# Routed experts: from 24 tiles of 256 slots with stationary weights to 39 tiles of 128 slots with stationary rows

## The reference, cut to what matters

```
probs = softmax(x @ router_w.T);  topk_w, topk_idx = top_k(probs, 2)   # x: 2048 x 512, 8 experts
topk_w = topk_w / sum(topk_w);    combine[token, expert] = topk_w
for each expert:                  # gate_w, up_w: 512 x 352; down_w: 352 x 512
    out = silu(x @ gw) * (x @ uw) @ dw
    acc = acc + combine[:, expert] * out
shared = silu(x @ s_gate_w + s_gate_b) * (x @ s_up_w + s_up_b) @ s_down_w + s_down_b
return acc + shared
```

## Time and profile before

| | us |
|---|---|
| median of 3 runs (2123.87 to 2126.93) | 2124.59 |
| the profiled execution | 2125.85 |
| its span, first to last instruction | 2124.1 |
| TensorE busy in the span | 1867.7 |

### The profile page before, as it was taken

One profiled execution on the slowest core, in us unless ns is written; L12 is line 12 of the kernel. 1 busy time (PEld: TensorE's weight loads), 2 busy tenths in 40 slices (PEclk: granted clock), 3 DMA queues, 4 the chain that ended last, 5 costly groups with the idle time before them and its releaser, 6 DMA issues. The chain is left out here.

```text
span 2124.1 us, 30631 instructions
## 1 busy us (share of the span) xinstructions
PE 1867.7 (88%) x11050; PEld 1539.2 (72%) x11050; DVE 1301.2 (61%) x2410; ACT 919.1 (43%) x1755; POOL 667.4 (31%) x482
## 2 busy tenths in 40 slices
PE   4999996965999679999999999984895999998597
PEld 4999984752445368888888888873674888987475
DVE  5343424777787447677767767755533777776244
ACT  3333323764667445465455536533212555553211
POOL 2110102214556321222213212102363666653322
PEclk8999997987999879999999999997997999999798
DMA  5010103541011331222213212003005777773434
GB/s 198 21 39 20 37 32 140 188 169 60 11 41 41 119 130 51 70 90 80 70 59 112 70 50 95 6 1 107 21 1 172 232 229 236 240 225 122 120 107 129
DMA packets 131028, 209.03 MB, mean 98 GB/s; under 512 B 9990, under 2 KB 69670, under 8 KB 130790
## 3 DMA queue, kind: packets, MB, share of 16 engines
q1 hardware_dynamic: 119228, 170.89, 24.0%
q0 software_dynamic: 11696, 36.77, 6.0%
HBM read 169.84 MB, written 37.79 MB: 98 GB/s over the span
## 5 line engine op out<-in xcount | busy, mean ns | idle before, releaser
L1311 POOL TENSOR_TENSOR a_rq<-a_ssq,a_mhalf 128x4 f32<-128x4 f32 x64 | 65.1, 1017 | 413.6 <-DVE a_ssq L1433 413.6
L69 PE MATMUL bank<-a_xT_hi,a_wq_lo 128*128 128x512 f32 (+1 forms) x384 | 145.0, 378 | 21.7 <-PEq L47 18.1
L1394 ACT ACTIVATE a_pT_hi<-bank 128x512 fp32r<-128x512 f32 x128 | 69.6, 599 | 192.9 <-PE bank L1548 192.9
L2222 DVE TENSOR_TENSOR m_h_lo<-m_hf,m_h_hi 128x256 fp32r<-128x256 f32 (+1 forms) x72 | 122.6, 1703 | 36.6 <-ACT m_h_hi L2176 36.6
L70 PE MATMUL bank<-a_xT_lo,a_wq_hi 128*128 128x512 f32 (+1 forms) x384 | 139.4, 363 | 0.0
L71 PE MATMUL bank<-a_xT_hi,a_wq_hi 128*128 128x512 f32 (+1 forms) x384 | 139.4, 363 | 0.0
L1388 ACT ACTIVATE a_scores<-a_scores,a_nmax 128x256 f32<-128x256 f32 x256 | 127.1, 503 | 27.9 <-DVE a_nmax L1448 27.6
L69 PE MATMUL bank<-a_wo_hi,a_oT_lo 128*128 128x512 f32 x320 | 128.2, 401 | 2.7 <-DVE a_oT_lo L368 1.4
L71 PE MATMUL bank<-a_wo_hi,a_oT_hi 128*128 128x512 f32 x320 | 126.5, 395 | 0.0
L70 PE MATMUL bank<-a_wo_lo,a_oT_hi 128*128 128x512 f32 x320 | 126.4, 395 | 0.0
L1441 DVE SCALAR_TENSOR_TENSOR a_scores<-bank,a_rq,a_mask 128x256 f32<-128x256 f32 x256 | 106.2, 478 | 32.3 <-PE bank L71 24.1
(11 more groups left out here) (410 smaller groups left out, 5955.9 us busy)
## 6 DMA issues: line engine op xcount, KB each, us to landing
m_graw<-in_egw SPq DMA_DIRECT2D x24, 704.0 KB, 5.0
m_uraw<-in_euw SPq DMA_DIRECT2D x24, 704.0 KB, 6.5
a_xT_hi<-x1T_hi SPq DMA_DIRECT2D x16, 1024.0 KB, 6.0
a_xT_lo<-x1T_lo SPq DMA_DIRECT2D x16, 1024.0 KB, 8.2
m_draw<-in_edw SPq DMA_DIRECT2D x24, 512.0 KB, 7.1
y_routed<-m_y SPq DMA_DIRECT2D x48, 256.0 KB, 3.9
m_draw<-in_edw SPq DMA_DIRECT2D x24, 192.0 KB, 7.3
a_cTraw<-in_ctxT SPq DMA_DIRECT2D x8, 512.0 KB, 3.4
```

Source lines behind the costliest of these rows:

```text
L69: pe.matmul(out, w[1], x[0], start=first, stop=False)
L1311: pool.tensor_tensor(rq[:, h % HG, :], ssq[:, h % HG, :], mhalf[:], ALU.pow).then_inc(s_rq, 1)
L1394: act.activation(pT[b].hi[:], ptb[b][:].rearrange("p (k s) -> p k s", k=QT), ACT.Copy).then_inc(ft.hi, 1)
L2222: dve.tensor_tensor(h.lo[r, m, :], hf[q][r, :], f32(h.hi[r, m, :]), ALU.subtract).then_inc(s_lo, 1)
```

## The change

Tiles are 128 slots wide, and 39 of them cover every split: NT = (4096 - 8) // 128 + 8 = 39. They are run in 24 groups, each with one load of weights: ND = 15 double groups (two tiles of one expert) and NS = 9 single ones. The order within each third is D S D D S D S D. Rows are stationary and weights move: a tile has 24 matmuls of 352 columns (4 k, gate and up, three products), whose result has slots on partitions, so that `hf` is transposed by TensorE (3 transposes) before the down projection (9 matmuls of 512 columns). The next rows take 4 transposes. `h_lo` becomes `hT_lo`, with one input in PSUM. SP's load of a group waits, as before, for the `lo` of the group two before it. All loops are unrolled. The router computes groups instead of tiles, with more VectorE steps; `position` comes before `slot`.

```
+    order = []
+    for n in range(3):
+        order += [(doubles[0], 2), (singles[0] + ND, 1), (doubles[1], 2), (doubles[2], 2), (singles[1] + ND, 1),
+                  (doubles[3], 2), (singles[2] + ND, 1), (doubles[4], 2)]
...
         @block.sync
...
+            load(0)
+            load(1)
+            for q in range(NG):
+                if q + 2 < NG:
+                    load(q + 2)
+                for n in range(begin[q], begin[q + 1]):
+                    store(n)
...
         @block.scalar
...
+            def split(q, n):
+                act.wait_ge(s_raw[j], at(q // 2 * 64 + 64))
...
+            for n in range(NT):
+                if n == begin[q] and q + 1 < NG:
+                    split(q + 1, 0)
+                if last and q + 1 < NG:
+                    split(q + 1, 1)
+                silu(n)
+                if n + 1 < NT:
+                    transposed(n + 1)
+                if last and q + 1 < NG:
+                    split(q + 1, 2)
+                hidden(n)
...
         @block.gpsimd
...
+            for q in range(NG):
+                for n in range(begin[q], begin[q + 1]):
+                    b = n - begin[q]
+                    if q + 1 < NG and b == 0:
+                        split(q + 1, 0)
+                    if n + XG - 1 < NT:
+                        gather(n + XG - 1)
+                    if q + 1 < NG and n + 1 == begin[q + 1]:
+                        split(q + 1, 1)
...
         @block.vector
...
+            transposed(0)
+            down_weights(0)
+            for n in range(NT):
+                gated(n)
+                if n + 1 < NT:
+                    transposed(n + 1)
+                if n >= 1:
+                    output(n - 1)
+                hidden(n)
+                if n + 1 == begin[q + 1] and q + 1 < NG:
+                    down_weights(q + 1)
...
         @block.tensor
...
+            for n in range(NT):
+                up(n)
+                if n + 1 < NT:
+                    transposed(n + 1)
+                if n >= 1:
+                    down(n - 1)
+                hidden(n)
+            down(NT - 1)
```

More of the change, by code:

```diff
@@ L1899, in positions @@
[L1899 to L1907, removed]
+                step(dve.tensor_reduce(rank[:], prod[:], AX.X, ALU.add))
@@ L1933, in _ @@
             hidden(1, 1)
-            first_tiles(a)
+            ends = first_groups(a)
             hidden(1, 2)
-            positions()
+            positions(ends)
             for t in chunk(1):
@@ L1939, in _ @@
             hidden(2, 0)
-            experts_of_tiles()
+            experts_of_groups(ends)
             hidden(2, 1)
@@ L2046, in routed_experts @@
     full, tail = I // P, MT[-1][1]
+    part_of = lambda n, of: range(n * ND // 3, (n + 1) * ND // 3) if of else range(n * NS // 3, (n + 1) * NS // 3)
+    order = []
+    for n in range(3):
+        doubles, singles = list(part_of(n, True)), list(part_of(n, False))
+        order += [(doubles[0], 2), (singles[0] + ND, 1), (doubles[1], 2), (doubles[2], 2), (singles[1] + ND, 1),
+                  (doubles[3], 2), (singles[2] + ND, 1), (doubles[4], 2)]
+    NG = len(order)
+    column = lambda g: 2 * g if g < ND else ND + g
+    tiles = [(q, column(g) + b) for q, (g, size) in enumerate(order) for b in range(size)]
+    NT = len(tiles)
+    begin = [next(n for n, (p, _) in enumerate(tiles) if p == q) for q in range(NG)] + [NT]
+    XG = 4
     with Phase(nc) as ctx:
@@ L2066, in routed_experts @@
[L2066 to L2070, removed]
-        s_st = [sem(f"y{j}_stored") for j in range(CT)]
+        xg = [sb(f"xg{j}", [P, D]) for j in range(XG)]
+        xT = [Pair(ctx, nc, f"m_xT{j}", [P, KD, P]) for j in range(2)]
@@ L2072, in routed_experts, with load @@
+        s_g, s_sg, s_u, s_h, s_y, s_yc = (sem(n) for n in ("gate", "silu", "up", "h", "down", "y_copied"))
+        s_st = [sem(f"y{j}_stored") for j in range(3)]
         ctx.start()
         block = ctx.enter_context(nc.Block())
[L2074 removed]
         @block.sync
         def _(sp):
[L2078 to L2082 removed]
+            def load(q):
+                j = q % 2
+                e = sp.value_load(group_expert[0:1, order[q][0]:order[q][0] + 1], min_val=0, max_val=E - 1)
+                if q >= 2:
+                    sp.wait_ge(s_wlo, at((q - 1) * 2))
+                    sp.wait_ge(s_dlo, at(q - 1))
```

408 lines of the change are left out of this document (195 added, 213 removed).

## The result

| | before | changed |
|---|---|---|
| median, us | 2124.9 (2123.87 to 2126.93, 4 runs) | 2159.49 (2156.6 to 2164.77, 4 runs) |
| ratio to before | | 1.0164 (95%: 1.014 to 1.0189) |
| profiled execution, us | 2125.85 | 2164.77 |
| first routed matmul to last, us | 333.9 | 364.9 |

The change costs 1.6%, 35 us. The forecast was 2132, range 2105 to 2152: the direction is right, the size is not. The same kernel measured again with the experiments gave 1.0163.

The account below looks back on a forecast made before the run. TensorE bounds the kernel before; after, late load landings bound the pairs. 2125.85 + 4.3 (routed stage) + 4 (clock) - 5.1 (stage start) + 4.5 (router) = 2133.6 us profiled, 2132 as median; range 2105 to 2152.

Parts of the forecast that it names:

- Which wait ends last: Routed stage, single group then double: the load issued behind the single's store lands last; the pair lasts 28.7 us.
- The size of the load: Weight load in the routed stage: 8.8 us from first issue to last landing, counted twice in a pair.
- The other doubles: Routed stage, double groups not behind a single: no stall to speak of, 13.55 us each, six of them 81.3.
- The clock: TensorE's clock falling to half in waits within pairs: 0.5 us a pair, +4 us in all, at most 11.
- Down weights' `lo`: VectorE's two-input subtraction meeting GpSimd: about 1 us a group, but nothing where the weight copy is late.
- TensorE's own sum: TensorE's work in the routed stage: 6.75 us a tile with switches, 263 us for 39 tiles, before 333.9.
- Start of the stage: Start of the routed stage: `xT_lo` comes first, so TensorE starts 5.1 us sooner (between 3 and 6).
- Router: Router: VectorE's additional steps ahead of the first addition are on the path, +4.5 us (from 2 to 6).
- sooner landing: Rival, routed stage: the load lands sooner or hand-overs are shorter, 2100 to 2123 us; chance 0.22.
- TensorE-bound: Rival, routed stage: loads land in time and TensorE bounds throughout, stage 285 us, time 2075 or 2057; chance 0.08.
- Slow code: Rival, routed stage: straight-line code must be fetched beside busier DMA engines, above 2150 us; chance 0.05.
- The clock rival: Rival: the clock falls in every pair and the slow tile delays the next chain, +7 to +15, 2139 to 2150; chance 0.15.

Follow-up runs that it names:

- e13: Changed kernel with idle matmuls where TensorE waits for `hf` (8 in each single group, 18 in the first tile of the double behind it): ratio to before 1.0188.
- e14: Changed kernel with the same idle matmuls in TensorE's waits for `hf`, and without the gathers of rows behind the first four: ratio to before 1.0062.
- e11: Changed kernel with a third raw weight buffer, and VectorE's down weights' subtraction left out behind the first two groups but for eight columns: ratio to before 0.9756.
- e4: Changed kernel without the 22 weight loads behind the first two and without ScalarE's wait for them: ratio to before 0.9818.
- e6: Changed kernel with a third set of raw weight buffers, so each load is issued one group earlier: ratio to before 0.9834.
- e10: Changed kernel with third raw buffer, first two router additions ahead of the position pieces, and single groups' gather behind both weight subtractions: ratio to before 0.9701.
- e5: The changed kernel itself, unaltered, measured again in the session of the experiments: ratio to before 1.0163.
- e7: Changed kernel with all gathers of rows behind the first four left out: ratio to before 1.0055.

## Why the prediction was right or wrong

- *Which wait ends last*: right. Store, load, ScalarE's copy, silu, TensorE, in this order and in the tiles named; nearly all of TensorE's idle time lies in the pairs.
- *The size of the load*: the step that failed. "It takes 1.7 + 7.1 = 8.8 us": 10.2 in the profiled execution. I took a landing measured in the kernel before, where the gathers start 3.5 to 5 us ahead of a load, and moved it to a place where one or two gathers of 256 KB run beside it. Under the rivals I had even named the gathers as a reason for a sooner landing. Without gathers it is 9.0. A smaller part was the reading: over all loads behind the first two, first issue to last landing is 9.05 us in the kernel before (8.4 to 10.7), not 8.8. Doubled, as "in a pair the load's time counts twice" says, 1.4 us make 2.8 a pair; measured are 2.4 over the sum with its 0.5 for the clock (by the pieces 1.55 in the single's load and 1.1 in the double's, less 0.25 in hand-overs).
- *The other doubles*: 13.55 predicted, 13.4 where the load is in time, 14.4 on average: three of the five are 13.4, the others 14.4 and 17.5, since the longer load no longer always fits behind 13.5 us.
- *The clock*: "I put 0.5 us a pair" is what e13 and e14 show, 0.4 to 0.6, and by the same reckoning: of 1.5 us in the second tile 1.0 comes back (2 and 1.45 in the forecast). Over a whole pair TensorE loses over 2.5 us gross. By the Trainium skill ("TensorE: Matmul & The Clock Gate", HAM oscillation) the clock falls at each wait for DMA in a kernel with little compute between them; the trace agrees (granted clock 0.50 from 1788 to 1792), and e13 adds that it is hardly paid where the next wait is longer.
- *Down weights' `lo`*: at nothing beside the late load, about 1 us a group otherwise, as written. With the load in time it costs 17 us in 22 groups (e11). Beside the late load it did meet GpSimd in the pair shown, 4.11 us for 1.21 from 1775.92, but VectorE's next work came only at 1788.37. The Trainium skill ("SBUF — State Buffer", SBUF: two separate sides) calls the pair of ports that VectorE and GpSimd share an exclusive lock, held for a whole instruction, when VectorE's work has two inputs in SBUF and GpSimd's reads SBUF; the 5.28 us row agrees that VectorE is blocked.
- *TensorE's own sum*: right. Matmuls of 352 columns start 0.16 us apart (predicted 0.158), a single group takes 6.8 us in e11 (6.75). Two of the changed kernel's, seven apart:

```profile
1984.71 0.32 PE L69 MATMUL bank<-m_wg_hi,m_xT_lo 128*128 128x352 f32 x1
...
1985.83 0.32 PE L70 MATMUL bank<-m_wg_lo,m_xT_hi 128*128 128x352 f32 x1
```

- *Start of the stage*: -4.7 for -5.1. *Last pair and end*: 25.5 for 24.6.
- *Router*: +6.8 for +4.5, above the 6 that I gave as its most. The rows are as summed (two of 768 columns 0.96 and 0.95): the first addition comes 8.6 us later than before, of which 3.9 were there already, which leaves +4.7. Left out was the clock. It falls over the wait of 5.4 us and is at half until 1555, and by the fourth addition (1546.43 before, 1557.13 now) the delay is +6.8, which no later wait takes back. The additions after:

```profile
1549.71 1.28 DVE L1823 TENSOR_TENSOR X<-X,bank 128x512 f32<-128x512 f32 x2
1554.76 0.69 DVE L1823 TENSOR_TENSOR X<-X,bank 128x512 f32<-128x512 f32 x1 [3.77 <-PE bank L71]
```

- *Rivals*: sooner landing is refuted. So is TensorE-bound (285 for the stage, 365 measured); without loads it is 293. Slow code is refuted by e4 and, with the loads, by e6 and e10. The clock rival (+7 to +15) named a real fall, but e13 prices it at the forecast's 0.5 us a pair. The remaining +3.9 and +1.9 us lie in stages that the change doesn't touch, and the profiled execution stands 5.3 us above its median where that of the kernel before stands 1 above; more I can't say of them.

## What to carry to other kernels

When stages shrink, look at the time at which each load is asked for, not at the bandwidth: a load issued behind a store that waits for the same load's consumer counts twice, and one more buffer removed the loss, since the DMA engines, full while a load runs, were idle between loads. Take a landing time from a stretch with the traffic that will be there, gathers included. After the bound is lifted, read the waits again: covers that were free (a shared lock, a gather in front of a subtraction) were worth about 0.8% each.

## What the runs showed of the hardware

- A half clock in front of a later DMA wait is nearly free: 11 us less of lost work in e13, 0.4 us a pair gained. In the router, where no later wait took it back, a half clock from about 1549 to 1555 cost 2.1 us.
- One gather of 256 KB just ahead of a load of 2.1 MB lengthens it by 0.9 us, two beside it by 1.6 us (e5 against e7). The DMA share was 0.57 from 1776 to 1807 us, but 1.04 to 1.07 while the loads ran.
- VectorE's two-input work can end behind the second of two back-to-back GpSimd subtractions: in e6 it waits out a subtraction that GpSimd started after it (1777.38 against 1778.33). In the e10 order, with a gather behind the subtractions, a pair is within 0.6 us of TensorE's own sum all the same.
- In the slower sessions TensorE stood for 1.5 to 2.2 us between single matmuls while GpSimd scattered, with no releaser in the trace (e5; in e6 up to 2.9 us). It is not in the first trace of the changed kernel, nor in that of e13, and its cause is open:

```profile
1579.11 0.59 PE L71 MATMUL bank<-r_xT_hi,r_wu_hi 128*96 128x512 f32 x1 [1.51 <-issue]
...
1584.04 0.59 PE L70 MATMUL bank<-r_xT_lo,r_wu_hi 128*96 128x512 f32 x1 [2.24 <-issue]
```
